# Four layers on one Trainium2 core: the order and issue of the work before the first scan

## The reference, cut to what matters

```python
h = tok(x, W, b)                          # patches (32, 36, 768) @ W.T + b
h = concatenate([h, txt], axis=1)         # (32, 68, 256)
# layer 0, mixer, on xn = layernorm(h):
z, params = xn @ W_z.T, xn @ W_params.T   # params: 64 of dt, C of 16 states
dt = softplus(dt_unproj @ W_dt.T + b_dt)
u  = silu(causal_conv(xn))
A_tilde, B_tilde = exp(dt * A), (A_tilde - 1) / A    # dt alone where |A| < 1e-5
h_t = A_tilde * h_(t-1) + B_tilde * u     # scan over 68 tokens, 16 states
y = (sum_n C_n h_n + u * D) * silu(z);  h = h + y @ W_out.T
# layer 1, feed-forward: weights composed from primitives
vals, idx = top_k(logits, 32); w = softmax(vals)      # of 64, for fc1 and fc2
W1 = einsum('k,kir,kro->io', w, A[idx], B[idx])       # and W2 likewise
```

## Time and profile before

| what | value |
|---|---|
| time, median of 3 runs (lowest to highest) | 1682.14 us (1678.66 to 1684.33) |
| profiled execution: its own time, span | 1694.94 us, 1693.1 us |
| PE, PEld, DVE, ACT, POOL busy | 92%, 66%, 47%, 30%, 26% of the span |
| mean granted clock of TensorE | 0.967 of full |
| moved by DMA | 142.13 MB, mean 84 GB/s |

### The profile page before, as it was taken

How to read it: one execution, slowest core, us unless ns; L and a number is a source line. 1 busy time by engine, 2 the same in 40 slices (tenths; PEclk the granted TensorE clock), 3 DMA queues, 4 the chain that set the end, 5 groups by cost and what they waited for, 6 DMA issues and landing times.

```text
span 1693.1 us, 22322 instructions
## 1 busy us (share of the span) xinstructions
PE 1561.7 (92%) x7798; PEld 1114.3 (66%) x7798; DVE 795.0 (47%) x1710; ACT 501.2 (30%) x983; POOL 434.8 (26%) x426
## 2 busy tenths in 40 slices
PE   5896898988899999999998999999999989998779
PEld 4542333448899999999996555778854445665664
DVE  3575798887111111111107773113766557667524
ACT  1246454441222221222214522113310025544210
POOL 0254687771111111111104000000010003222350
PEclk9998999998999999999999997999999999999889
DMA  5233554445355555321312002001000010001231
GB/s 177 63 104 98 138 126 105 110 92 179 126 193 212 212 205 195 121 82 51 147 44 78 1 0 84 0 1 50 1 1 0 1 50 1 11 1 38 89 108 63
DMA packets 63366, 142.13 MB, mean 84 GB/s; under 512 B 11244, under 2 KB 41605, under 8 KB 56549
## 3 DMA queue, kind: packets, MB, share of 16 engines
q1 hardware_dynamic: 56884, 122.46, 22.7%
q0 software_dynamic: 6368, 18.23, 3.3%
HBM read 205.26 MB, written 15.61 MB: 130 GB/s over the span
## 4 chain that ended last, share of the span: by engine, by line
PE 75%; DVE 13%; issue 3%; ACT 2%; POOL 2%; DMA 2%; SPq 1%; another core or an unknown queue 1%; DVEq 0%; POOLq 0%; ACTq 0%
PE psum L810 43%; PE psum L1134 9%; PE psum L842 7%; PE psum L905 4%; DVE work L1880 3%; PE psum L1050 2%; PE psum L820 2%; DVE work L2020 1%; DVE work L2019 1%; POOL work L2113 1%; PE psum L969 1%; DVE bst L1535 1%; PE psum L988 1%; DMA work<-in_txt 1%; PE psum L1174 1%
## 5 line engine op out<-in xcount | busy, mean ns | idle before, releaser
L810 PE MATMUL psum<-work 128*128 128x128 f32 (+3 forms) x3400 | 471.2, 300 | 15.6 <-DMA work<-in_xp 15.6
L810 PEld LDWEIGHTS psum<-work 128*128 128x128 f32 x3400 | 441.3, 193 | 32.5 <-DMA work<-in_xp 15.6
L1947 DVE TENSOR_TENSOR work<-sq,psum 128x512 f32<-128x512 f32 x82 | 56.3, 687 | 390.6 <-PE psum L810 390.6
L2113 POOL TENSOR_TENSOR work<-work,w_late 128x408 f32<-128x408 f32 (+1 forms) x160 | 162.4, 1050 | 53.9 <-DVE work L1880 24.4
L1880 DVE TENSOR_TENSOR_SCAN work<-psum,work 128x414 f32<-128x414 f32 (+1 forms) x160 | 159.7, 1060 | 34.5 <-POOL work L2113 22.6
L2077 POOL TENSOR_TENSOR rs<-rs,power 128x4 f32<-128x4 f32 (+3 forms) x40 | 44.4, 1112 | 480.3 <-DVE rs L1542 472.4
L905 PE MATMUL psum<-work,xn 128*128 128x408 f32 (+1 forms) x320 | 148.4, 575 | 15.9 <-POOL work L2113 15.4
L1134 PE MATMUL psum<-w_late,xn 128*128 128x512 f32 x352 | 153.9, 595 | 0.0
L2139 POOL DMA_INDIRECT y_rows<-sq,row_of x41 | 40.6, 990 | 361.7 <-ACT sq L1234 361.7
L1335 ACT ACTIVATE psum<-work,a_neg 128x408 f32<-128x408 f32 (+1 forms) x160 | 100.0, 627 | 105.2 <-DVE work L1880 105.2
L905 PEld LDWEIGHTS psum<-work,xn 128*128 128x128 f32 x320 | 53.6, 193 | 105.0 <-POOL work L2113 86.2
(11 more groups left out here) (284 smaller groups left out, 2097.1 us busy)
## 6 DMA issues: line engine op xcount, KB each, us to landing
work<-in_W SPq DMA_DIRECT2D x123, 1024.0 KB
w_late<-c_rows SPq DMA_DIRECT2D x48, 204.0 KB, 3.5
w_attn<-in_B SPq DMA_DIRECT2D x64, 128.0 KB, 2.5
w_late<-c_rows SPq DMA_DIRECT2D x32, 238.0 KB, 3.7
w_attn<-in_A SPq DMA_DIRECT2D x64, 64.0 KB, 2.2
w_attn<-in_A SPq DMA_DIRECT2D x32, 128.0 KB, 2.5
work<-y_rows SPq DMA_DIRECT2D x8, 512.0 KB, 6.9
w_late<-in_we SPq DMA_DIRECT2D x2, 2048.0 KB, 8.3
```

The costliest lines, as they stand in the source:

```text
L810: mm = pe.matmul(dst, lhs(k), rhs(k), start=(k == 0), stop=(k == parts - 1))
L1947: dve.tensor_tensor(hm[:, j % 2, 4 * q:4 * q + 4, :].rearrange("p k n -> p (k n)"), sa[:, i % 2], A.at(("e3", j, q)), ALU.mult).then_inc(s ...
L2113: pool.tensor_tensor(seqs(ym[:, g % RING, 0:ntok(c)]), f[:, :, 1:SEQ + 1], seqs(cbr[:, k % CRING, 0:ntok(c)]), ALU.mult).then_inc(sem("y_p ...
```

## The change: what it does

1. The ten tables are issued by ScalarE. SP issues token weights, pixels of chunk 0, bias, text, and then the other pixels.
2. TensorE's `tok` of a chunk is placed before the `hT` of the chunk before it; the primitives' sum and weights become two steps, after chunk 0 and after chunk 1.
3. VectorE does the primitives' chain before the guard constants.
4. Long and short part of a primitive lie side by side in memory and are one transfer.
5. Units 0, 1, 2 stand behind `ln` of duos 0, 2, 4, and GpSimd scales them before the powers of the norm; units 3 to 5 stand where the six stood.
6. C goes out behind unit 17, and the first four C rows come in behind unit 19.
7. ScalarE keeps the first composed pass before it splits dt of the last chunk. VectorE computes the step sizes inside the branch, which is thus taken earlier.

```diff
+FIRST_UNITS = 3
-        for c in range(CHUNKS):
+        def plan_tok(c):
             for m in range(HALVES):
                 F.plan(("tok", c, m), (sem("tok_kept"), 2 * c + m + 1))
             step("tok", c)
+        plan_tok(0)
+        F.plan(("prim_sum",), (sem("setup_step"), 1))
+        step("prim_sum")
+        for c in range(CHUNKS):
+            if c + 1 < CHUNKS:
+                plan_tok(c + 1)
+            if c == 0:
+                F.plan(("prim_w",), (sem("prim_w_kept"), 2))
+                step("prim_w")
             for d in DUOS_OF[c]:
                 F.plan(("hT", d), (h_ready, H(0, d)))
                 step("hT", d)
-            if c == 0:
-                F.plan(("prim_sum",), (sem("setup_step"), 1))
-                F.plan(("prim_w",), (sem("prim_w_kept"), 2))
-                step("prims")
...
-        plan_ln(L0A, range(DUOS))
+        for d in range(DUOS):
+            plan_ln(L0A, [d])
+            if d % 2 == 0 and d < 2 * FIRST_UNITS:
+                plan_units(1)
         step("guards")
-        plan_units(6)
+        plan_units(6 - FIRST_UNITS)
...
     SP: the ten loads that signal prim_loaded are gone (ScalarE has them, ahead of its first wait)
             load(wtok, "wtok", "tok_loaded")
-            load(tokb[:], "tokb", "tok_loaded")
             sp.dma_start(xp[:, :, 0:first_img], ...)
+            load(tokb[:], "tokb", "tok_loaded")
+            load(txt, "txt", "txt_loaded")
             sp.dma_start(xp[:, :, first_img:], ...)
-            load(txt, "txt", "txt_loaded")
...
-                    for dst, name in ((unit_long(i), ...), (unit_short(i), ...)):
-                        sp.dma_start(dst[rows, :], t[name][bass.DynSlice(prim, 1)]...)
+                    sp.dma_start(unit_tile(i)[rows, :], t[f"unit{p}"][bass.DynSlice(prim, 1)]...)
...
             for i in range(EARLY):
                 load_unit(i)
-            sp.wait_ge(sem("par_kept"), CHUNKS)
-            sp.dma_start(c_rows, pc[DT_RANK:DT_RANK + N_STATE, :]).then_inc(sem("c_stored"), 16)
-            sp.wait_ge(sem("c_stored"), 16)
+                if i == PAIRS + 1:
+                    sp.wait_ge(sem("par_kept"), CHUNKS)
+                    sp.dma_start(c_rows, pc[DT_RANK:DT_RANK + N_STATE, :]).then_inc(sem("c_stored"), 16)
+                if i == PAIRS + 3:
+                    sp.wait_ge(sem("c_stored"), 16)
+                    for k in range(CRING):
+                        load_c(k)
             for k in range(CHUNKS * N_STATE):
-                load_c(k)
+                if k >= CRING:
+                    load_c(k)
...
     ScalarE
+            keep_comp(0)
             split_dt(CHUNKS - 1)
...
-            keep_comp(0)
...
     VectorE: primitives' chain ahead of the guard constants; the loop over the step sizes
     becomes step_sizes()
             def scans(general):
+                step_sizes()
...
     GpSimd
-            ln(L0A)
             pool.wait_ge(sem("prim_w_kept"), 2)
-            scale_units(0, PAIRS - 2 * CHUNKS)
+            scale_units(0, FIRST_UNITS)
+            ln(L0A)
+            scale_units(FIRST_UNITS, PAIRS - 2 * CHUNKS)
```

More of the change, by code:

```diff
@@ L275, in build @@
         late_slots += [xn_flat[:, r * (PHALF + D):(r + 1) * (PHALF + D)] for r in range(PAIRS - XTOK_SLOTS)]
+        unit_tile = lambda i: slots[i % PSLOTS] if i < BRIDGE else late_slots[i - BRIDGE]
         unit_long = lambda i: tile_long[i % PSLOTS] if i < BRIDGE else late_slots[i - BRIDGE][:, 0:PHALF]
@@ L698, in load_unit @@
                     rows = slice(w * RANK, (w + 1) * RANK)
-                    for dst, name in ((unit_long(i), ("B1", "A2")[f] + f"_{p % 2}"), (unit_short(i), ("A1", "B2")[f])):
-                        sp.dma_start(dst[rows, :], t[name][bass.DynSlice(prim, 1)].rearrange("e p n -> (e p) n")).then_inc(
-                            unit_loaded(i)[0], 16)
+                    sp.dma_start(unit_tile(i)[rows, :], t[f"unit{p}"][bass.DynSlice(prim, 1)].rearrange(
+                        "e p n -> (e p) n")).then_inc(unit_loaded(i)[0], 16)
             def load_c(k):
@@ L863, in prims, with prim_w @@
                           stop=True).then_inc(sem("setup_sums"), 1)
+            def prim_w():
                 pe.wait_ge(sem("setup_step"), 2)
@@ L1247, in router_act @@
                     copy(gT[:, 4 * P * j:4 * P * j + n], W8.at(("gateT", r, j))[0:EXPERTS, 0:n], "gateT_kept")
+            for dst, name in ((lower, "lower"), (krow, "krow"), (half, "half"), (pidx, "pidx"), (alog, "alog")):
+                act.dma_start(dst[:], t[name]).then_inc(sem("prim_loaded"), 16)
+            act.dma_start(a_t[DT_RANK:DT_RANK + N_STATE, 0, :], t["alogT"]).then_inc(sem("prim_loaded"), 16)
+            for f, name in enumerate(("fc1_logits", "fc2_logits")):
+                act.dma_start(prow[:, f, :], t[name + "_row"].to_broadcast([PRIMS, PRIMS])).then_inc(
+                    sem("prim_loaded"), 16)
+                act.dma_start(pcol[:, f, 0:1], t[name + "_col"]).then_inc(sem("prim_loaded"), 16)
             act.wait_ge(sem("prim_loaded"), 10 * 16)
@@ L1784, in _ @@
             dve.memset(power[:], -0.5).then_inc(sem("dve_setup"), 1)
+            dve.wait_ge(sem("prim_loaded"), 10 * 16)
+            for f in range(2):
+                lcol = pcol[:, f, 0:1]
+                link(dve.tensor_scalar(ptmp[:, f], prow[:, f], lcol, None, ALU.is_equal))
+                link(dve.tensor_tensor(ptmp[:, f], ptmp[:, f], lower[:], ALU.mult))
+                link(dve.tensor_scalar(ptmp2[:, f], prow[:, f], lcol, None, ALU.is_gt))
+                link(dve.tensor_tensor(ptmp[:, f], ptmp[:, f], ptmp2[:, f], ALU.add))
+                link(dve.tensor_reduce(pcol[:, f, 4:5], ptmp[:, f], AX_X, ALU.add))
+                link(dve.tensor_scalar(pcol[:, f, 5:6], pcol[:, f, 4:5], float(TOP_PRIMS), None, ALU.is_lt))
+                link(dve.tensor_scalar(ptmp2[:, f, 0:TOP_PRIMS], krow[:], pcol[:, f, 4:5], None, ALU.is_equal))
+                link(dve.tensor_reduce(pcol[:, f, 6:7], prow[:, f], AX_X, ALU.max))
+                link(dve.tensor_tensor(pcol[:, f, 1:2], pcol[:, f, 0:1], pcol[:, f, 6:7], ALU.subtract))
+            dve.tensor_copy(pcol[:, :, 7], pcol[:, :, 1]).then_inc(sem("dve_setup"), 1)
+            dve.wait_ge(sem("act_setup"), 2)
+            dve.tensor_tensor(pcol[:, :, 3], pcol[:, :, 2], pcol[:, :, 5], ALU.mult).then_inc(sem("dve_setup"), 1)
             dve.wait_ge(sem("act_setup"), 1)
@@ L1842, in _, with step_sizes @@
             ins.then_inc(sem("diag_ready"), 1)
-            for c in range(CHUNKS):
-                for m in range(HALVES):
-                    g, n = 2 * c + m, ntok(c)
-                    dve.wait_ge(sem("dt_ln"), g + 1)
-                    r, l = seqs(dt_pos[:, m, chunk(c)]), seqs(sp_a[:, g % 2, 0:n])
-                    d = seqs(dtx[:, m, chunk(c)])
-                    dve.tensor_tensor(d[:, :, 1:SEQ], r[:, :, 0:SEQ - 1], l[:, :, 0:SEQ - 1], ALU.add)
-                    dve.tensor_tensor(d[:, :, 0:1], r[:, :, 0:1], l[:, :, 0:1], ALU.add).then_inc(sem("dt_ready"), 1)
+            def step_sizes():
+                for c in range(CHUNKS):
+                    for m in range(HALVES):
+                        g, n = 2 * c + m, ntok(c)
+                        dve.wait_ge(sem("dt_ln"), g + 1)
+                        r, l = seqs(dt_pos[:, m, chunk(c)]), seqs(sp_a[:, g % 2, 0:n])
+                        d = seqs(dtx[:, m, chunk(c)])
+                        dve.tensor_tensor(d[:, :, 1:SEQ], r[:, :, 0:SEQ - 1], l[:, :, 0:SEQ - 1], ALU.add)
+                        dve.tensor_tensor(d[:, :, 0:1], r[:, :, 0:1], l[:, :, 0:1], ALU.add).then_inc(sem("dt_ready"), 1)
             def scan(g, general):
```

48 lines of the change are left out of this document (13 added, 35 removed).

## The result

| | median | lowest to highest | runs |
|---|---|---|---|
| before | 1680.80 us | 1678.66 to 1684.33 | 4 |
| changed | 1652.68 us | 1649.97 to 1657.02 | 4 |

The ratio is 0.9832 (95% interval 0.9806 to 0.9859): 28 us less. A second measurement, of the same kernel with five runs, gave 0.9818 (0.9795 to 0.9842), 30.6 us less. The forecast was 1649.7.

A forecast was written before the change was run, and what follows sets the result against it. The prediction saw five different limits in the first 371 us, with the scan at VectorE's pace. Terms -11.4 - 0.4 + 0.8 - 6.6 - 4.0 - 3.3 - 7.5 = -32.4 took 1682.14 to 1649.7; 8-of-10 range 1641 to 1667.

The forecast's parts named there:

- the first chunk: First chunk of the scan: SP needs 3.10 us per row and unit for 4.40; -7.5 us, bounds 0 and -11.
- Tables from ScalarE: Start of the kernel: second token chunk starts at 19.3 for 30.71; -11.4 us.
- rival (d): Start of the kernel: large transfers and tables delay each other, pixels land at 22.4; +3.1 us, 1653, inside forecast's range.
- Tokens a chunk ahead: Token stage: TensorE's waits for ScalarE's copies go, -2.4; primitives' weights and a transpose group come in, +2.0; -0.4 us.
- The norm's end: End of the first norm: VectorE becomes the bound, giving back +0.8 us; three scalings on GpSimd cost nothing.
- Three units between: Before the z stage: three of six units lie in TensorE's waits for VectorE; -6.6 us, bounds -4 and -7.2.
- Rival (a): SP's queue: one larger transfer costs SP what the pair did; +10.3 us, 1660, chance 0.14.
- C rows early: Start of the scan: the pause between third and fourth scan goes; -4.0 us, bounds 0 and -4.0.
- keep_comp and the branch: Before the first scan: copies move ahead of split_dt, branch moves over idle time; -3.3 us, bounds -1 and -3.7.
- Rival (b): First chunk of the scan: TensorE becomes the bound once C rows are in time; 1659 us, chance 0.16.
- Rival (c): Scan: TensorE stays at its lower clock; 1694 us if through both chunks, chance 0.04.
- From 204.6 on the same work in the same time: After the first gating: nothing changes, though faster unit loads there may give 1 us.

The follow-up runs named there:

- again: The changed kernel itself, unaltered, run a second time for a tighter time and a second profile: 1653.95 us, ratio 0.9818.

## Why the prediction was right, step by step

The total came from the right stages: 32.7 for 32.4 us at the first gating. That it is so close is in part luck: the first term was 2.2 us too large, and the tokens, the units between and the first chunk together gave 2.3 more than forecast. One term was given to one edit where it hangs on three.

- **Tables from ScalarE, -11.4 (measured -9.2).** The failed piece is the bound "landing slowly behind large transfers, about 12 us": the last table landed at 16.1. From there the 4.8 us of VectorE that the prediction had hidden beside the first token chunk led to prim_sum at 21.12, which held TensorE 4.43 us. That the pixels land at 19.3 was right (19.56 once nothing else held the chunk), so rival (d), pixels at 22.4, is not what happened. With the tables back on SP the chunk started at 23.53: issue by ScalarE is worth 2.1 us in the changed kernel and, against the kernel with prim_sum moved, 4.0. The other 7.1 of the 9.2 are order, and not earlier pixels: with the tables on SP these landed at 23.5, for 22.4 before. Chunk 1 no longer stands behind the text, which landed at 24.94 before and was there for GpSimd at 11.76 here; with TensorE's old order (the run with the tokens behind) it still started at 22.61. The prediction's "first operation came at 8.49" overlooks a table load of ScalarE at 0.73, which now runs behind the ten issues, at 7.63, and cost nothing, since the tables were not in. The Trainium skill (DMA: Bandwidth & Descriptors, "Issuing engines are not separate DMA queues") says that a second issuer saves issue time and shares the engines. The runs agree: ScalarE's small transfers took 8.8 us beside the large ones and 2.3 alone. I had used that rule for the large transfers and not for the small, on which the chain hung.
- **Tokens a chunk ahead, -0.4 (measured -1.4, again -0.2).** TensorE waited 0.62 to 0.65 us for each of the four copies before, as reckoned at 0.6. The two profiles of the changed kernel differ by the clock in the second chunk, so this term's size is not settled by them. In the run that undoes it the last h-transpose is 2.2 to 3.4 later; z only 1.4 to 2.6, since the norm's end is VectorE's.
- **The norm's end, +0.8 (+0.4).** The three scalings on GpSimd (0.92 to 0.94 us, at 35.37, 37.28 and 39.51) did not all lie where VectorE waited, as the prediction has it: the first two ran beside its statistics and copies. These took 0.75 and 0.68 to 0.69 us as before, so no blocking shows. The units landed later than reckoned, and GpSimd was free at 40.43 for 38.1. That cost nothing either: VectorE came to its first norm operation at 42.11 without a wait for GpSimd.
- **Three units between, -6.6 (-7.0; undone +6.5 to +7.7).** They cost the transposes nothing that shows, and they ran at the full clock: the grant was 1.00 in this stretch, for 0.84 and 0.85.
- **One transfer per primitive.** 1.24 us per primitive measured for 1.22, and a period of 3.12 for 3.10. Rival (a) is out.
- **C rows early, -4.0; and the first chunk, -7.5.** Together 11.5; measured 4.0 and 8.5, together 12.5. But the 4.0 do not belong to the early rows alone, as the sum has it. In the changed kernel, leaving the C rows last cost nothing. The merge alone, in the kernel before, gave 11.6 at the first gating, 2.7 of them at that pause, with the rows late; and undoing it brought 2.28 of pause back, with the rows early. The step counts its units at 2.45, that is with the merge, and gives all of it to the row that the wait named. The prediction also had the 9.9 us by which TensorE's second half of units starts earlier "off the path". By the traces it is on it: SP's slots, and behind them C, hung on these units, and with keep_comp moved C goes out 12.7 us ahead of its product even when it comes last. This was read from the traces; how the 1.27 us that the merge alone leaves are shared between keep_comp and the earlier z stage was not tested. Nor are the early rows shown to be useless on their own: before, GpSimd was done with its last unit at 152.52 and stood for the row till 155.97, so that in that kernel an earlier row would have been worth up to 3.4 us of the pause, by estimate from these two times.
- **Rival (a), priced 10.3.** The run that undoes the merge has its condition, and cost 14.7 at the gating, 16.8 at the scan's end and about 14 in time (1667.74 against 1653 to 1654). Its +2.2 for the late last unit was right (2.28). Too low were the later start (2.5, where the first scan came 3.9 later) and the rest of the first chunk (5.6, where 10.85 less the 2.28 are 8.6).
- **keep_comp and the branch, -3.3.** From z to the first scan 3.0 were saved; the branch and the edges are 1.7 of these, 2.5 had been reckoned. The part of keep_comp was not run alone.
- **Rival (b), TensorE in the first chunk.** TensorE had 37.5 of 42.2 us, and GpSimd waited for it 0.30 and 0.56 us. It was a small cost, not the bound. Rival (c), a lasting lower clock, did not come: grant 0.96 in the first chunk.
- **"From 204.6 on the same work in the same time."** Not quite. Chunks 2 to 4 took 124.9 us for 122.8 (from the gating at 213.47 to that at 338.32, and from 246.12 to 368.94), and the saving fell from 32.7 to 30.6. Chunk 4 took 36.77 at a grant of 1.00 before, 37.84 at 0.95 here, 36.2 at 1.00 with the tables on SP, 39.2 at 0.91 without units between. So the length goes with the grant. What makes the grant dip in one chunk and not in another was not tested.
- The prediction took the saving off the median of the runs and not off the profiled execution. That mattered: the profile of before holds waits of 8.7 us in the last layer that no later profile showed.

The separate parts don't add up to the whole in the medians: undone one at a time, only the merge shows (14 us of 28 to 31). The others are 2 to 7 us at z and 0 to 3 in the time, each within its interval.

## What to carry to other kernels

When an engine waits for a transfer, look at what its queue issued in front of it, and at what that waited for in turn. Here the wait named a C row. The row stood on SP behind two units, these behind TensorE's slots, and TensorE behind two copies on ScalarE. Cheaper unit transfers took 2.7 us of that pause, and with the whole queue earlier the row's own place in it no longer mattered.

What an edit is worth depends on which others are in. The early C rows are worth nothing in the changed kernel, and in the kernel before an estimate gives them up to 3.4 us. So undo an edit in the new kernel and also put it alone into the old one; only the merge had both runs, and it was worth 14 us either way.

Small transfers on which a chain hangs should be in before the large ones start, or the chain's first reader should stand behind other work.

The Trainium skill (DMA: Bandwidth & Descriptors, "Rules for kernel authors") advises to coalesce small transfers and sees mostly overhead below 64 KB. Here pairs of 128 and 64 KB were still worth merging, since an issue slot of the one engine that issues them was what ran out.

## What the runs showed of the hardware that was not expected

- 0.2 KB landed in 2.3 us alone and in 8.8 us (median of two; the last 9.09) beside 5.2 MB of large transfers.
- A 192 KB transfer took SP 1.24 us with the read of its address, where 128 and 64 KB took 1.87 together, and landed in 3.0 us.
- SP's issue slots were uneven while the large transfers were under way: in the changed kernel's first 20 us those of `wout` and `jrow` took 2.47 and 2.48 us, and others 0.4 to 0.6.
- The second token chunk's 24 matmuls took 5.37 us at a granted clock of 1.00, where TensorE had stood 1.33 us before them; 7.05 at 0.76 behind 2.33 and 2.70; 6.88 at 0.78 behind 4.43; 8.08 at 0.66 behind 4.96. So an earlier start behind a longer wait gave part of itself back. The first chunk's 24, of the same shape, took 7.0 to 8.4 us in the thirteen profiles, at a recorded grant of 1.00 in the eight where it was read; why is open.
